# Transposing 128x1024 fp16 row tiles by transfers instead of by TensorE, in a cross-attention and mixture-of-experts kernel

## The reference, cut to what matters

```python
x = x + xattn(layernorm(x), ctx, ctx, Wq, Wk, Wv, Wfc, bfc)    # 32 heads, 8 key/value groups
h = layernorm(x)                                              # the "normed rows", (2048, 512)
scores = softmax(h @ gate_weight.T)                           # 8 experts
topk_w, topk_i = group_limited_topk(scores)                   # best 2 of 4 groups, then best 2
g, u = einsum('th,nfh->ntf', h, gate_w), einsum('th,nfh->ntf', h, up_w)      # f = 352
e = einsum('ntf,nhf->nth', silu(g) * u, down_w)
routed = einsum('nth,tn->th', e, wmat)                        # wmat: topk_w at topk_i
shared = silu(h @ sh_gate_w.T) * (h @ sh_up_w.T) @ sh_down_w.T               # 704 wide
x = x + routed + shared
```

## Time and profile before

| | us |
|---|---|
| three runs | 829.26 median, 827.61 to 833.52 |
| the profiled execution | 835.35, its span 833.6 |
| PE busy | 800.4 (96%), 5498 matmuls |
| DVE busy | 598.7 (72%) |
| ACT busy | 446.6 (54%) |
| POOL busy | 269.6 (32%) |
| granted TensorE clock, mean | 0.991 |
| chain that ended last | PE 83%, DVE 7%, ACT 4%, DMA 3%, issue 2%, another core or an unknown queue 1% |
| DMA | 149.10 MB, mean 179 GB/s |

### The profile page before, as it was taken

The page is one execution under the profiler, slowest core; times in us unless marked ns, Lnnn a source line. Parts: engine busy times, 40 slices in busy tenths (PEclk is TensorE's granted clock), DMA queues, the critical chain, the costliest instruction groups (busy, mean ns, idle before and its releaser), DMA issues.

```text
span 833.6 us, 17091 instructions
## 1 busy us (share of the span) xinstructions
PE 800.4 (96%) x5498; PEld 448.6 (54%) x5499; DVE 598.7 (72%) x1226; ACT 446.6 (54%) x876; POOL 269.6 (32%) x224
## 2 busy tenths in 40 slices
PE   6999999999999989999999999999999999989996
PEld 3453533334433246566666666666666666646663
DVE  4767789999999769986897856556555555536665
ACT  2655589999999935665446533333333333323332
POOL 3352029999964006652001011111111110032331
PEclk9999999999999999999999999999999999999998
DMA  8997755565556889985722332222223222165663
GB/s 310 366 344 238 234 200 166 180 189 192 157 150 206 316 324 315 372 280 178 302 77 84 109 102 87 75 88 88 75 84 92 75 78 86 39 202 177 193 200 124
DMA packets 68676, 149.10 MB, mean 179 GB/s; under 512 B 10704, under 2 KB 24528, under 8 KB 67984
## 3 DMA queue, kind: packets, MB, share of 16 engines
q1 hardware_dynamic: 57436, 106.99, 37.5%
q0 software_dynamic: 11120, 41.43, 15.8%
q10 hardware_dynamic: 68, 0.02, 0.0%
HBM read 105.40 MB, written 42.73 MB: 178 GB/s over the span
## 4 chain that ended last, share of the span: by engine, by line
PE 83%; DVE 7%; ACT 4%; DMA 3%; issue 2%; SPq 1%; another core or an unknown queue 1%; DVEq 0%; ACTq 0%
PE psum L1386 29%; PE psum L1400 17%; PE psum L1228 8%; PE psum L1214 7%; PE psum L1144 4%; PE psum L1314 4%; PE psum L1120 3%; PE psum L1376 3%; PE psum L1245 2%; PE psum L1485 2%; DMA sb_weights<-attn_dram 1%; ACT sb_weights L952 1%; DMA sb_weights<-in_wqT 1%; PE psum L1101 1%; PE psum L1096 1%
## 5 line engine op out<-in xcount | busy, mean ns | idle before, releaser
L1386 PE MATMUL psum<-sb_weights,sb_rows 128*128 (+1 forms) x1608 | 263.4, 314 | 0.0
L1386 PEld LDWEIGHTS psum<-sb_weights,sb_rows 128*128 128x128 f16 x1608 | 158.0, 98 | 78.0
L952 ACT ACTIVATE sb_weights<-psum,sb_rows 128x512 f32<-128x512 f32 x256 | 158.3, 684 | 15.8 <-PE psum L1214 14.0
L1400 PE MATMUL psum<-sb_weights,sb_hT 128*128 (+1 forms) x639 | 150.9, 382 | 2.3 <-DVE sb_hT L1866 2.3
L1605 DVE TENSOR_REDUCE sb_rows<-psum 128x4 f32<-128x1024 f32 x128 | 149.8, 1213 | 4.3 <-PE psum L1144 4.3
L829 POOL DMA_INDIRECT sb_rows<-xn_rows,sb_slot_tok x39 | 38.4, 983 | 251.1 <-PE psum L1485 207.4
L1022 ACT ACTIVATE psum<-sb_h 128x352 f32<-128x352 f32 x71 | 33.2, 468 | 125.8 <-DVE sb_h L1848 122.4
L1400 PEld LDWEIGHTS psum<-sb_weights,sb_hT 128*128 128x128 f16 x639 | 62.7, 98 | 69.1 <-DVE sb_hT L1866 2.6
L1034 ACT CAST sb_hT<-psum 128x384 f16<-128x384 f32 x71 | 34.0, 479 | 122.0 <-PE psum L1376 110.4
L1866 DVE TENSOR_TENSOR sb_hT<-psum,sb_hT 128x384 f16<-128x384 f32 x71 | 39.4, 555 | 79.2 <-ACT sb_hT L1034 77.6
L1214 PE MATMUL psum<-sb_weights 50*128 50x512 f16 x256 | 89.6, 388 | 3.0 <-ACT sb_weights L952 2.6
(11 more groups left out here) (254 smaller groups left out, 1128.8 us busy)
## 6 DMA issues: line engine op xcount, KB each, us to landing
sb_weights<-in_wgu SPq DMA_DIRECT2D x20, 704.0 KB, 6.8
sb_weights<-in_wgu POOLq DMA_DIRECT2D x20, 704.0 KB, 5.1
sb_weights<-in_wdn SPq DMA_DIRECT2D x17, 768.0 KB, 6.7
slot_y<-sb_rows SPq DMA_DIRECT2D x39, 256.0 KB, 2.0
sb_weights<-q_parts SPq DMA_DIRECT2D x96, 64.0 KB, 2.3
x_dram<-sb_rows SPq DMA_DIRECT2D x24, 256.0 KB, 2.7
sb_weights<-in_x SPq DMA_DIRECT2D x4, 1024.0 KB, 7.3
q_parts<-sb_weights SPq DMA_DIRECT2D x16, 256.0 KB, 4.4
```

The costliest lines, as they stand in the source:

```text
L952: nc.scalar.activation(probs[G % 2][:, kt, pair * 512:(pair + 1) * 512], bank[4 + f % 2], ACT.Exp, scale=exp_scale[:, n:n + 1]).then_inc(e ...
L1386: mm = nc.tensor.matmul(bank[GU_BANKS[par][which]][:, 0:F], x_T[:, xp * D + k * P:xp * D + (k + 1) * P], gu(wp, k, which), start=(k == 0 a ...
L1400: mm = nc.tensor.matmul(bank[Y_BANKS[par]][:], hT[par][:, hp, j, :], dn(wp, j), start=(j == 0 and n == 0), stop=(j == NF - 1 and n == 2))
```

## The change

1. The normed rows are scaled while they are normalised and cut in the row layout: ScalarE copies the high half (`rows_high`), VectorE subtracts for the low half (`rows_low`), both into `xn16[s]`, 128 x 1024 fp16. That is stored as `xn2_rows`, now (T, 1024) fp16; `xnT_dram` is gone.
2. `ln_transpose`, `lnt_out` and `cut_rows` are gone. The gate's operand comes from a transposing transfer from SBUF to SBUF (`dma_start(..., transpose=True)` on SP), the gate weight is cut into fp16 halves too, and the gate is 8 fp16 matmuls (4 of 16 columns, 4 of 8). The logits' two parts are added in `softmax_in`.
3. Early and late tiles are loaded from `xn2_rows` by transposing transfers.
4. Gathers of the slots bring fp16 halves (2 KB a row, as before). `slot_transpose` and `slot_evac` are gone; SP transposes the gathered rows into xT by a transfer (`slot_rows`), and VectorE copies only the slot's two factors (`slot_inv`). `gather_slot` waits for the transfer that empties its buffer.
5. All ten held low halves and the two shared down ones are made by VectorE; GpSimd only issues their loads.
6. The late gathers of pairs 1, 2 and 3 wait for `u_ready` of late units.
7. SP's loops over tiles and slots are written out in place of hardware loops.

```diff
@@ SP, token stage
-            def store_lnT(t, s):
-                sp.wait_ge(ln16_done, t + 1)
-                sp.dma_start(tile_of(xnT_dram, t), ln16[s]).then_inc(lnt_stored[s], 16)
-            def store_xn2(t, s):
-                sp.wait_ge(ln2_done, t + 1)
-                sp.dma_start(tile_of(xn2_dram, t), xn2_sb[s]).then_inc(xn2_stored[s], 16)
+            def by_column(rows_T):
+                return rows_T.rearrange("p (k t) -> p k t", t=P)
+            def store_rows(t, s, read=None):
+                sp.wait_ge(xn_cut, t + 1)
+                sp.dma_start(tile_of(xn2_dram, t), xn16[s]).then_inc(xn2_stored[s], 16)
+                if read is not None:
+                    sp.wait_ge(gate_ready, read)
+                sp.dma_start(by_column(gate_xT[s]), xn16[s], transpose=True).then_inc(gate_ld[s], 16)
@@ SP, shared tiles and slots
-                sp.dma_start(xT[s], tile_of(xnT_dram, t)).then_inc(sx_ld[s], 16)
+                sp.dma_start(by_column(xT[s]), tile_of(xn2_dram, t), transpose=True).then_inc(sx_ld[s], 16)
+            def slot_rows(m, s, n, free):
+                sp.wait_ge(slot_ld[s], n * 16 + 16)
+                sp.wait_ge(u_ready, free)
+                sp.dma_start(by_column(xT[s]), slot_in[s], transpose=True).then_inc(sx_ld[s], 16)
-            with sp.Fori(0, SLOTS // 2) as i:
+            for i in range(SLOTS // 2 - 1):
                 for s in range(2):
+                    slot_rows(i * 2 + (s + 2), s, i + 1, i * 2 + (s + B0 + 1))
                     store_slots(i * 2 + s, s)
@@ GpSimd
-                    pool.wait_ge(xt_ready, m - 1)
+                    pool.wait_ge(sx_ld[m % 2], SX_SEEN + 16 * (m // 2))
...
                 if q >= 4:
                     pool.wait_ge(out_st[buf], OUT_SEEN[buf] + 16 * (q // 4))
+                elif q > 0:
+                    pool.wait_ge(u_ready, C0 + 2 + q)
@@ ScalarE
-                nc.scalar.activation(ln16[s][:, 0:D], bank[4 + s][:], ACT.Copy, scale=X_SCALE)
-                nc.scalar.copy(lnT[s], bank[4 + s][:]).then_inc(lnt_evac, 1)
+            def rows_high(t, s):
+                act.wait_ge(ln2_done, t + 1)
+                act.wait_ge(xn2_stored[s], t // 2 * 16 + FREE)
+                if t >= 2:
+                    act.wait_ge(gate_ld[s], t // 2 * 16)
+                nc.scalar.copy(xn16[s][:, 0:D], xn2_sb[s]).then_inc(xn_high, 1)
@@ TensorE
-                for k in range(KD):
-                    mm = nc.tensor.matmul(bank[6 + s][:, 0:NE], lnT[s][:, k * P:(k + 1) * P], gw_sb[:, k, :], ...
+                for part in range(2):
+                    for k in range(KD):
+                        x_k = gate_xT[s][:, part * D + k * P:part * D + (k + 1) * P]
+                        if part == 0:
+                            mm = nc.tensor.matmul(bank[4 + s][:, 0:2 * NE], x_k, gw16[:, k].rearrange("p a e -> p (a e)"), ...
+                        else:
+                            mm = nc.tensor.matmul(bank[4 + s][:, 0:NE], x_k, gw16[:, k, 0, :], ...
...
-            def slot_transpose(m, s, n):
-                ...
-            def slot_up(m, s):
-                pe.wait_ge(xt_evac, m + 1)
+            def slot_up(m, s, n):
+                pe.wait_ge(sx_ld[s], n * 16 + (16 + SX_SEEN))
+                pe.wait_ge(inv_ready, m + 1)
                 gate_up(m + B0, s, xT[s], routed_gu(m))
@@ VectorE
-                nc.vector.scalar_tensor_tensor(ln16[s][:, D:2 * D], bank[4 + s], X_SCALE, ln16[s][:, 0:D],
-                                               ALU.mult, ALU.subtract).then_inc(ln16_done, 1)
+                nc.vector.tensor_tensor(xn16[s][:, D:2 * D], xn2_sb[s], xn16[s][:, 0:D], ALU.subtract).then_inc(xn_cut, 1)
...
             for t in range(2, TILES):
                 residual_norm(t, t % 2, t // 2)
-                if t % 2 == 1 and t < 2 * HELD + 2:
+                if t == 2:
+                    gate_second()
+                if t < 2 * HELD + 2:
                     second_part(t - 2)
+                elif t - 2 * HELD - 3 in range(SH):
+                    dn_second_shared(t - 2 * HELD - 3)
```

More of the change, by code:

```diff
@@ L273, in build @@
         cmp_b = rows[:, 6 * D:8 * D]
-        h_sb = [sb(f"h{i}", [P, FP]) for i in range(2)]
         hT = [sb(f"hT{i}", [P, 2, NF, P], F16) for i in range(2)]
@@ L567, in _, with token_tile @@
                 load_res_rows(1, t)
-                store_xn2(t, t)
-            def token_tile(i, s, more=True):
+            store_rows(0, 0)
+            def token_tile(i, s, more=True, read=True):
                 if more:
@@ L668, in _ @@
                     load_res(m + s * EARLY, 2 * m + s)
-            with sp.Fori(0, EARLY // 2 - 1) as i:
+            for i in range(EARLY // 2 - 1):
                 for r in range(2):
@@ L853, in _ @@
         def _(act):
[L855 removed]
+            for stored in parts_st:
                 act.sem_inc(stored, FREE)
@@ L980, in _ @@
             ot_evac(0, 0)
-            for t in range(2):
-                ot_evac(t + 1, (t + 1) % 2)
-                std2(t)
             def dn_first(e, pieces):
```

259 lines of the change are left out of this document (113 added, 146 removed).

## The result

The changed kernel takes 841.09 us (median of 4 runs, 839.56 to 844.25) against 829.46 us of kernel before (4 runs, 827.61 to 833.52): ratio 1.0132, 95% interval 1.0103 to 1.0162. The forecast was 808 us, range 800 to 853. The value lies inside the range, but on the other side of kernel before. In a second set it was 842.83 us against 835.70, ratio 1.0047, interval 1.0009 to 1.0086. Both intervals lie above 1: slower, by 0.1 to 1.6%. Ratios are of runs at most 1.5% above the fastest of their kernel; e4 has one such run of four, and e8 three (its fourth took 1289.5 us). The profiled execution took 841.88 us, its span 840.0 us.

What follows compares the result with a forecast made beforehand. TensorE chains were taken to bound the slots, with TensorE, VectorE and DMA limits close together in the token stage. From the median: 829.26 - 17.2 (slots) - 2.0 (token stage) - 2.6 (half the accident) = 807.5, stated as 808 us, range 800 to 853.

Steps and rivals of the forecast that it cites:

- the token stage: 311 to 382 us: VectorE still sets the pace, 2.0 us gained; new transfers cost nothing, at the far end 10 us.
- Rival C: Token stage: slots as forecast, but the stage is bound by full DMA engines, +10 us, 820 us in all; chance 0.10.
- rival A: Slots: slow transposing transfer and SP's place make slots wait, 854 us, over 1000 in the worst form; chance 0.27.
- VectorE's side of the ten tiles: Token stage, tiles 2 to 12: 5.33 us a tile plus 0.3 for the gate's second half, 53.6 us against 54.7.
- Slots: Slot stage: 39 slots lose four TensorE transposes of 0.44 us each, 17.2 us gained, all kept at period 5.85 us.
- L: Slots: time from issue to landing of the transposing transfer, taken as 3.7 us.
- The threshold: Slots: the period stays 5.85 us while the transposing transfer lands within 4.3 us of its issue.
- The forecast's own formula: Slots: above the threshold the period is (7.4 + L)/2, so L is twice the period less 7.4.
- Accident: Near 738 us, VectorE's pause beside a gather burst: spacing the gathers removes it, 5.2 us; half, 2.6, counted from the median.
- rival D: Late units: spacing the gathers does not cure the accident or moves it, 811 us; chance 0.49 together with the forecast.
- Early and late tiles, route: Transposing loads issued 11.7 us ahead of use, and one added 0.3 us VectorE instruction beside slack: zero cost.
- the worst form of rival A: Slots: eight 128x128 blocks handled one after another; over 1000 us, or some 935 at 1309 ns a block; chance 0.06.

Runs made afterwards that it cites:

- e4: Kernel after with the attention-row loads of tiles 3 to 15 issued by ScalarE on its own queue instead of SP: 842.0 us.
- e8: As e7, but pairs 1 to 7 of the last gathers each wait for a late unit, in place of pairs 1 to 3: 816.3 us, ratio 0.9711.
- f3: e2 plus a second transposing transfer (128x768) for tiles 2 to 11, which the gate waits for but nothing reads: 826.3 us, ratio 0.9931.
- e2: Kernel after with held loads 3 to 9 cut to 16 columns each, transposing transfers kept: 827.1 us, ratio 0.9902.
- e7: Kernel after with TensorE transposing the gate operand, slot stores one step later in SP's queue, slot 2's transfer earlier, two late loads later: 816.7 us, ratio 0.9750.
- e1: Kernel after with the gate operand moved by a plain copy of the same bytes instead of the transposing transfer: 828.2 us, ratio 0.9906.
- g1: Kernel after with the gate operand transposed by TensorE, plus nine transposing transfers in the token stage that nobody reads: 843.0 us, ratio 1.0061.
- f1: Kernel after with the gate operand's transposing transfer cut to the high half, which the gate reads twice: 826.3 us, ratio 0.9938.
- f4: As e7, but each of pairs 1 to 15 of the last gathers waits for a late unit: 813.3 us, ratio 0.9784.
- f5: Kernel before with only pairs 1 to 15 of the last gathers each made to wait for a late unit: 832.6 us, ratio 0.9964.
- g3: The same kernel as f4, run again beside before and after: 815.5 us, ratio 0.9753.

## Why the prediction was wrong

**The step that failed is the token stage**: "Nothing at all is my value, 10 us the far end". The stage was to give -2.0 us and came out at +17.3 from tile 2 to the first down product (98.51 us against 81.25), 15.8 of it on tiles 2 to 12. The forecast weighed the transfer by its work on the DMA engines (room 1.0 us a tile, at worst 2 us of them) and by its landing time in a quiet stage. Both sizes were fair: the work is at most 1.6 us (f3), the landing 3.2 to 6.3 us without company (e2). What it had no term for is that transposing transfers and 704 KB loads in flight together slow each other, and all others, to a third of the rate for up to 8 us at a time. That the bytes stay the same proved to be no argument. Rival C named the place and a mechanism (DMA engines full), with +10 and a chance of 0.10; the place was right, the size some two thirds, and the mechanism only in part. That 841 us lies inside the range is luck: the range reached so far for rival A, slow transfers in the slots, and it was filled by the token stage. VectorE's side of the ten tiles was right: 5.33 us a tile, GpSimd's arithmetic gone, the gate 0.35 us. The end of the stage was not: a gain of 0.3 us was forecast for the first shared unit, and from tile 15's x2 to the first down product it takes 11.9 to 14.4 us in every kernel with the new stage, where it took 10.6.

**Slots.** L was taken as 3.7 us and measured 3.6. The threshold was wrong: 4.3 us left out what lies between the landing and the first matmul, 0.8 to 1.2 us in this trace. So a period of 5.85 needs a landing within about 3.4 us, not 4.3 (an estimate: 3.1 to 3.2 us leave 1.4, of which about 1.1 is needed), and 3.8 us gives some 6.15. 21 of the 39 landings are longer than 3.4, so 36 periods gave 9.4 of the 15.8 us that were theirs. The forecast's own formula, twice the period less 7.4, gives 4.6 us for the mean period of 6.01: the median landing and a microsecond. e7 takes the transfer out from behind the store and gives the rest back.

**Handover.** The forecast counted what SP does in a slot period and not what stands ahead of slot 2's transfer: a base store that waits, and two late loads, 1.30 and 1.23 us to issue, the second of which waits for the landing of that store. +4.0 us, in no term.

**Accident.** Gone in the profiled execution (-5.4 us), as forecast, but not cured: rival D had it right. The waits move the burst by three pairs, and in seven of eleven traces of kernels with these waits the pause is there, at 1.9 to 5 us. The one trace was lucky.

**Early and late tiles, route:** nothing, as forecast: all early and late units keep their periods.

By the traces: +18.6 - 1.5 + 4.0 - 9.4 - 5.4 = +6.3 us, the difference of the two spans (6.4). The medians differ by 11.6, because the profiled execution of before was 5.9 us above its median.

By the Trainium skill's page "Advanced Engine Details and Errata", section "X-Bar Transpose (TRN2)", transposing transfers are as fast as regular ones. In the slots the transfer takes a median of 3.6 us where the plain store took 2.0, and beside the held loads 13.1 us where the plain copy of the same rows in e1 took 6.8 to 7.2, so it does not hold here. The Trainium skill's page "VectorE: DVE Perf Modes", section "The three transpose paths", has 1309 ns for one 128x128 block. Added up for eight, as the worst form of rival A did, that is no price here: all eight land in 3.0 us at best.

## What to carry to other kernels

Before putting transposing transfers into a stage, look at what else is in flight there: in a quiet stage 128x1024 in fp16 costs 1.3 us of its queue and 3 to 4.5 us to land, beside loads of 704 KB one can make a tile 5 to 11 us longer. Read the GB/s beside the DMA share: a share of 1 or more at 359, at 262 and at 117 GB/s are three different things, and e2 had 1.03 with nothing lost. In a queue that alternates a transfer with a store that waits, compare the whole distribution of landing times with the threshold, add the microsecond from the landing to the first matmul, move the store one step back, and walk through the first and last rounds. A wait that spaces the first of a row of gathers moves the burst to where the waits end.

## What the runs showed of the hardware

- Between the landing of a transfer and TensorE's first matmul on it, with TensorE standing ready, lay 1.19 us at the handover and 0.8 to 1.2 us in the slots for which it stood.
- Beside large loads the issue of a transposing transfer itself took SP up to 9.60 us (g1), against medians of 1.24 (e7) and 1.30 us (after) in the slots.
- Transposing transfers and 704 KB loads together: 117 GB/s on busy engines for 8 us, packets of both 2 to 4 times slower. Half the transposing bytes (f1): 341 GB/s over 320 to 360 us and nearly nothing lost.
- The DMA share does not say what room is left: it read 1.03 and 1.04 for 53.5 and 54.2 us of the same ten tiles, with 1 and 1.75 transposing transfers a tile.
- VectorE stood still for 2.5 to 5.7 us beside some eight indirect gathers that GpSimd issued in a row, in most traces but not in all; beside two to four in a row it did not in the three traces that have that (f4, f5, g3).
